# Layer two's expert tiles in a new order on three engines, and four of the eight gather buffers in other columns

## The reference

```python
logits = x @ router_w                        # 32 experts
probs = softmax(logits); topw, topi = top_k(probs, 4)
combine[t, topi] += topw / sum(topw)
g = einsum('th,ehi->eti', x, w_gate)         # 256 -> 96 per expert
u = einsum('th,ehi->eti', x, w_up)
routed = einsum('eti,te,eih->th', silu(g) * u, combine, w_down)
return shared + routed                       # shared: a dense two-layer branch
```

## Time and profile before

| | |
|---|---|
| median of three runs | 428.37 us |
| lowest and highest | 427.02 and 430.78 us |
| span of the profiled execution, first to last instruction | 462.5 us |
| TensorE busy | 421.1 us, 91% |
| VectorE, ScalarE, GpSimd busy | 329.8, 234.4, 216.2 us |
| first gate/up to the end of the tiles of layer two | 294.76 to 385.09 us |

### The profile page before, as it was taken

One profiled execution on the slowest core, in us unless ns is written; L12 is line 12 of the kernel. 1 busy time (PEld: TensorE's weight loads), 2 busy tenths in 40 slices (PEclk: granted clock), 3 DMA queues, 4 the chain that ended last, 5 costly groups with the idle time before them and its releaser, 6 DMA issues.

```text
span 462.5 us, 10086 instructions
## 1 busy us (share of the span) xinstructions
PE 421.1 (91%) x3213; PEld 327.6 (71%) x3213; DVE 329.8 (71%) x1135; ACT 234.4 (51%) x596; POOL 216.2 (47%) x208
## 2 busy tenths in 40 slices
PE   8899999899999998998989899958988999969696
PEld 4757899798999997656666684646766774645585
DVE  5886699978866667588999988525576664344685
ACT  3373233434433436878899636315566568124421
POOL 2023688767643320778880101655576602747400
PEclk9999999999999999589999999979999999979889
DMA  8937888888999982379776760233555523323202
GB/s 246 409 142 240 319 275 268 250 258 279 282 312 308 316 277 69 79 195 211 150 172 187 268 210 7 85 87 114 166 145 149 165 92 116 107 63 104 68 23 68
DMA packets 42274, 84.17 MB, mean 182 GB/s; under 512 B 7136, under 2 KB 27104, under 8 KB 41584
## 3 DMA queue, kind: packets, MB, share of 16 engines
q1 hardware_dynamic: 30656, 60.99, 39.6%
q0 software_dynamic: 9936, 20.85, 18.5%
q10 hardware_dynamic: 1632, 1.71, 1.1%
HBM read 65.81 MB, written 15.60 MB: 176 GB/s over the span
## 4 chain that ended last, share of the span: by engine, by line
PE 63%; DVE 14%; issue 8%; ACT 6%; another core or an unknown queue 4%; DMA 3%; SPq 1%; POOL 1%; ACTq 0%; DVEq 0%
PE ps L1169 14%; PE ps L1120 7%; PE ps L1185 7%; PE ps L1147 4%; PE ps L1289 4%; PE ps L964 3%; PE ps L1264 3%; PE ps L1106 3%; PE ps L1377 3%; ACT til L835 2%; PE ps L948 2%; PE ps L967 2%; DMA experts<-in_gu 2%; PE ps L1158 2%
## 5 line engine op out<-in xcount | busy, mean ns | idle before, releaser
L544 POOL DMA_INDIRECT til<-xn_rows,gidx x71 | 71.0, 999 | 98.1 <-PE ps L1158 43.4
L1169 PEld LDWEIGHTS ps<-til,experts 128*128 128x128 f32 x752 | 90.6, 192 | 8.1 <-issue 3.9
L1169 PE MATMUL ps<-til,experts 128*128 128x128 f32 x752 | 92.1, 276 | 3.2 <-DVE til L1645 1.5
L708 ACT ACTIVATE til<-ps 128x256 f32<-128x256 f32 x47 | 18.0, 382 | 66.2 <-PE ps L1158 66.2
L835 ACT ACTIVATE til<-til,mxs 128x128 f32<-128x128 f32 (+1 forms) x128 | 49.0, 453 | 0.0
L1185 PE MATMUL ps<-experts,til 128*128 x188 | 48.4, 381 | 0.0
L1120 PE MATMUL ps<-experts,til 128*64 x192 | 36.1, 345 | 9.4 <-issue 9.4
L756 ACT ACTIVATE til<-ps,wtile 128x256 f32<-128x256 f32 x95 | 42.0, 471 | 2.5 <-PE ps L1149 2.4
L1769 DVE CUSTOM_DVE_ANT_0 til<-ps,cst 128x128 f32<-128x128 f32 (+1 forms) x128 | 37.8, 352 | 5.7 <-PE ps L1264 3.3
L1120 PEld LDWEIGHTS ps<-experts,til 128*64 128x64 f32 x192 | 26.7, 144 | 15.5 <-issue 12.2
L1122 PE MATMUL ps<-xn,til 128*64 128x192 f32 x192 | 36.2, 345 | 0.0
(11 more groups left out here) (240 smaller groups left out, 959.4 us busy)
## 6 DMA issues: line engine op xcount, KB each, us to landing
experts<-in_gu SPq DMA_DIRECT2D x47, 512.0 KB
sorted_rows<-til SPq DMA_DIRECT2D x95, 128.0 KB
experts<-in_gu SPq DMA_DIRECT2D x8, 768.0 KB
experts<-in_dn SPq DMA_DIRECT2D x4, 1024.0 KB, 11.0
experts<-in_dn SPq DMA_DIRECT2D x8, 384.0 KB
experts<-att SPq DMA_DIRECT2D x44, 32.0 KB
til<-xn_rows,gidx POOLq DMA_INDIRECT x71
xr<-in_x SPq DMA_DIRECT2D x2, 512.0 KB, 4.2
```

Source lines behind the costliest of these rows:

```text
L544: po.indirect_dma_start(to, None, xn_dram[s.n], bass.IndirectOffsetOnAxis(ap=gidx[:, t:t + 1], axis=0))\
L1169: mm = pe.matmul(ps[:, b0, m * P:(m + 1) * P], gw[:, j, k * w + m * P:k * w + (m + 1) * P], xgT[:, j % 2, k, :], start=(k == 0), stop=(k = ...
```

## The change

Three things are changed.

- TensorE's order. The list is replaced by a loop that is written out: in step g gate/up of g, turn of g+1, down of g-1, the registers of g+1, turn-hidden of g. Beside before, T(g+1) and D(g-1) change places, and the register load moves behind D.
- The lists of ScalarE and VectorE. ScalarE's turn copies now run one group ahead, right behind the `silu` of the group; both weighings and both down copies stand together. VectorE makes the down copies and adds the biases ahead of the group's products of gate and up.
- The four gather buffers in `wqkv_sb` are given up. Tiles 4 to 7 of each eight go to the mask's columns of `cst`, to `bias_bf`, to `lgt` and to a new tensor `xg_more` of 1 KB per partition. Gather 4 waits for two counts of the block before (`s_wo`, `s_mx`) in place of `wide_done`.

```diff
-        xg1 = [xg[:, n, :] for n in range(4)] + [wqkv_free[:, n * D:(n + 1) * D] for n in range(4)]
+        xg1 = [xg[:, n, :] for n in range(4)]
...
+        xg_more = sb("xg_more", [P, D])
...
+        xg1 += [cst[:, C_MASK:C_MASK + D], bias_bf.bitcast(f32)[:, 0:D], lgt[:, :], xg_more[:, :]]
...
-                    if 0 <= g - lag < NT1 // 4:
+                    if max(0, -lag) <= g - lag < NT1 // 4:
                         work(g - lag)
...
                         if t == 4:
-                            po.wait_ge(s.wide_done, NTT)
+                            po.wait_ge(s_wo, BATCH)
+                            po.wait_ge(s_mx, 2 * BATCH * HEADS)
...
-                    run_double_tiles([(0, turn_four), (1, copy_second), (2, weigh_second), (0, gate_four), (2, silu_rows), (1, weigh_first), (0, copy_first)])
+                    turn_four(0)
+                    run_double_tiles([(2, weigh_second), (1, copy_first), (1, copy_second), (2, silu_rows), (0, gate_four), (-1, turn_four), (1, weigh_first)])
...
-                    run_double_tiles([(0, experts_of_four), (0, turn_four), (1, turn_h_four), (0, up_four), (1, down_four)])
+                    groups = NT1 // 4
+                    experts_of_four(0)
+                    turn_four(0)
+                    for g in range(groups):
+                        up_four(g)
+                        if g + 1 < groups:
+                            turn_four(g + 1)
+                        if g >= 1:
+                            down_four(g - 1)
+                        if g + 1 < groups:
+                            experts_of_four(g + 1)
+                        turn_h_four(g)
+                    down_four(groups - 1)
...
-                    run_double_tiles([(0, first_copies), (1, turned_four), (0, gate_four), (0, copy_four), (1, biases), (3, products)])
+                    run_double_tiles([(0, first_copies), (1, turned_four), (1, copy_four), (1, biases), (0, gate_four), (3, products)])
```

More of the change, by code:

```diff
@@ L167, in build_program @@
         gu_second = [xn_free[:, n * 384:(n + 1) * 384] for n in range(4)]
-        wqkv_free = wqkv_sb[:, :, :].rearrange("p k n -> p (k n)")
-        xg1 = [xg[:, n, :] for n in range(4)] + [wqkv_free[:, n * D:(n + 1) * D] for n in range(4)]
+        xg1 = [xg[:, n, :] for n in range(4)]
         dn_second = [wo0_sb[0:F1, n, :] for n in range(2)] + [xn_free[0:F1, 1536 + n * D:1536 + (n + 1) * D] for n in range(2)]
```

## The result

The changed kernel takes 430.46 us (median of 20 runs, 427.75 to 436.19); the kernel before took 428.40 us in the 20 runs beside it (425.84 to 432.33). The ratio is 1.0047 (1.0030 to 1.0065): slower by 2.0 us, 1.3 to 2.8. That is inside the range given, and on the other side of no change than the forecast. It is less than the 1% that the prediction took as what a measurement can tell from no change; with 20 runs of each, the interval tells it from no change all the same.

What follows compares the result with a forecast made beforehand. It took late TensorE signals, 0.91 to 0.94 us in each of eight layer-two groups, as the loss in the profile, mostly absent when timed. 428.4 - 1.1 - 1.0 + 0.2 = 426.5 us; range 419.2 to 432.5.

Steps and rivals of the forecast that it cites:

- the opening: Start of layer two's tiles: gathers 4 to 7 start sooner without the projections' wait; 1.0 us won, bounds 0 and 2.4.
- the freezes: TensorE's signals of finished tiles 1.5 us late beside gathers in layer two, costing 0.91 to 0.94 us a group.
- Nothing is added or removed: TensorE's order in layer two's groups: turn and down only change places, so the swap itself adds no time.
- The steady gain: Layer two's eight steady groups: gap ahead of gate/up closes, 7.4 us at full price, 1.1 at share 0.15.
- the 34.1 us between profile and clock: Profiled span 462.5 us against 428.37 timed; taken as mostly unexplained time that timed runs lack.
- Rival B: Layer two's groups: the freezes are real in full in timed runs, giving 420.2 us; chance 0.27.
- C: Layer two's gathers: real freezes, more of them with continuous gathers; 435.7 us, or 432.8 at six tenths; chance 0.12.
- rival E: Whole kernel: no effect, the end and gate/up's other wait take back the opening's 1.0; 428.4 us; chance 0.08.
- ScalarE's list: Weighings and down copies behind turn copies: hidden in groups, 0.2 us lost at the last down, bounds 0 and 0.8.
- VectorE's list: Biases and down copies ahead of the product turn-hidden needs; they fit ahead of gate/up's silu, so nothing.
- Rival D: Layer two's groups: gathers become the bound, 8.0 us a group if all are long, 444.9 us; chance 0.03.
- A: Whole kernel: the forecast itself, 426.5 us, own range 424 to 428.5; chance 0.50.

Runs made afterwards that it cites:

- e4: Kernel before with only the new gather buffers and the waits for gathers 4 to 7; ratio 0.9983 (0.9950 to 1.0015).
- e9: Kernel before with only the new gather buffers and waits, run a second time; 428.24 us, ratio 0.9995 (0.9971 to 1.0019).
- e2: Changed kernel with down put back ahead of turn on TensorE, new lists and buffers kept; ratio 1.0009 (0.9978 to 1.0041).
- e1: Kernel before, unedited, profiled once more; ratio 0.9999 (0.9967 to 1.0031), span 428.1 us.
- e7: Changed kernel again, unedited; 431.06 us, ratio 1.0068 (1.0037 to 1.0100).
- e3: Changed kernel with the old gather buffers and the old wait for the projections, new orders kept; ratio 1.0084 (1.0052 to 1.0116).
- e5: Changed kernel with TensorE's turn and down in halves of two tiles, down first; ratio 1.0045 (1.0014 to 1.0075).
- e6: Changed kernel with TensorE's turn and down in halves of two tiles, turn first; ratio 1.0105 (1.0073 to 1.0138).
- e10: Changed kernel a third time, unedited, on the same chip as e9; 431.41 us, ratio 1.0065 (1.0037 to 1.0093).

## Why the prediction was right or wrong

**The sum.** Two more changes of the array's use in each of ten groups cost 10 x 0.24 = 2.4 us, the tail 0.6, and the opening gives back 1.3: +1.7 us against 2.0 measured (1.3 to 2.8). By e4 and e9 the opening's gain may be less in the timed runs, which puts the sum between 1.7 and 3.0. A long gather 3 would add 1.4 in the executions that have it, and the agreement doesn't exclude some of those. I had -1.9: of the 3.9 us between that and the result, 2.4 are the changes of the array's use, 1.1 the freezes that weren't there and 0.4 the tail; the opening gave 0.3 more than expected. That leaves 0.3 unexplained, which is inside the interval.

**The step that failed** is the first of the parts, "Nothing is added or removed", for T ahead of D on TensorE. I counted instructions, and these are indeed the same; I took "D and its change-over" as one block that changes its place. But a change-over belongs to a pair of neighbours, not to a block. The old order has one behind D and one ahead of U, and none between U and D; the new one has two more, between U and T and between T and D. The trace of before had the price in it: the distance from the last gate/up to the first down and that from the last down to the first turn differ, and I read only starts of stages there. In numbers the term was 0 and is 2.4 us. Without it the traces sum to 1.3 - 0.6 = 0.7 us faster, the direction of the forecast; e2 is that kernel, and its times (1.0009, 0.9978 to 1.0041) can't be told from no change. TensorE has no idle time in these groups that could take it up, so it went to the time in full.

The Trainium skill has the rule: "TensorEngine Tiling (Array Packing)", section "Key Properties", says that changing the tiling mode, and not just the tile, drains TensorE. The traces agree in that each such change costs 0.12 to 0.15 us; that it is a drain no row shows. I hadn't weighed it, and it speaks against this change.

**The steady gain.** Expected 1.1 us from freezes paid at 0.15, with 0 and 7.4 as ends. Measured: none, as the second trace of before has groups of 5.98 us. The inference from the 34.1 us between profile and clock was right in kind, and its end 0 was the true one. What I set wrong was to take a trace that differed by 34 us as a picture of the kernel with a share to be scaled, when it was another kind of execution altogether. Against e1 its 34.4 us more are 6.2 ahead of T(0), 14.6 in the tiles (90.33 and 75.72) and 13.6 behind them (77.4 and 63.8). Rival B (0.27) falls for all usual executions, and so does C, which needed real freezes: its side came true, by another mechanism. That the result lies inside the whole range is luck for the same reason: what lies above 428.5 in it stands there for C's price, which nobody paid. The time lies 2 us above the forecast's own range (424 to 428.5) and nearest to rival E, no effect (428.4); E's reasons, that the end and another wait of U take the opening's gain back, hold for the tail only. By the page of the Trainium skill that the prediction cites here, "NOTIFIC — the notification-queue block", section "Overflow: three behaviours, one of which stalls the engine", the writing of records can stall an engine, which gives share 0. The share 0 came true, but no row shows this cause: e1 was recorded in the same way and has no freezes.

**The opening.** Expected 1.0, from 0.7 to 1.4; 1.3 in the traces. The step was right: the landing left the path. Gather 4 came 1.36 us behind gather 3 in e7 and e9, as worked out (1.06 and 0.30), in place of 3.76. But it then took 2.1 us itself where 0.94 was assumed, so gather 7 started 6.27 us behind gather 3 in e9 and 7.52 in e1, 1.25 us sooner and not 2.4. That was still enough for the wait of 1.2.

**ScalarE's list.** Hidden in the steady groups, as said (e2). The tail: bounds 0 and 0.8, 0.2 taken, 0.58 measured. I had argued that TensorE has only H(11) to cover it, which was the reason to stay near the upper end; I took the lower without a row.

**VectorE's list.** Taken as nothing. So it is in the steady groups. In the tail its down copies stand behind the copies of the hidden rows, end 0.05 us later than ScalarE's, and are what the last down waits for. By these two times either list alone should give nearly all of the 0.58; no run has only one of them.

One reading was off without consequence: the turn copies start at 363.90, 0.8 us and not 0.7 after T's last matmul began (363.08, the next row at 363.19 less 0.11).

**Rival D**, gathers as the bound: no. POOL is busy for 4.71 us of 6.23, and the gathers are as long as in the old order.

**The signs.** T stands right behind U and D behind T: seen. Groups of 6.0 us: 6.22. Second silu late: no, since there are no freezes. A span near 454 beside times near 426.5 as a sign for A: 427.2 beside 430.5, because a sign that rests on the trace of one odd execution has no worth for the next.

## What to carry to other kernels

When stages change places on an engine, count the borders between them as well as the stages: here every border between matmuls on part of the array and on the whole costs 0.12 to 0.15 us, though TensorE shows as busy throughout, so stages of one kind stand best side by side, and a reorder that closes an idle time must win more than its borders. Before a row of a trace is read, hold its span against the timed runs; where they differ by more than a few us, take another trace first, since a share of a rare event can't be scaled. At the end of a pipeline, where the cover runs out, list for every engine what stands ahead of the last wait.

## What the runs showed of the hardware

**A gather of two lengths.** Gather 3 starts while VectorE is in an unbroken train of sixteen fp16 products (279.78 to 283.35 in the changed kernel). In GpSimd's timeline of that trace, gathers 3 and 4:

```profile
280.71 3.46 POOL L546 DMA_INDIRECT til<-xn_rows,gidx  x1 [0.30 <-issue]
284.48 0.95 POOL L546 DMA_INDIRECT cst<-xn_rows,gidx  x1 [0.30 <-issue]
```

In e7, the same program, the same two:

```profile
283.12 1.05 POOL L546 DMA_INDIRECT til<-xn_rows,gidx  x1 [0.30 <-issue]
284.48 2.11 POOL L546 DMA_INDIRECT cst<-xn_rows,gidx  x1 [0.30 <-issue]
```

Either gather 3 takes 3.46 us or gather 4, where it is issued there, takes 2.11; both end 0.8 us behind the end of the train (283.35; in e7 285.76). When it is the third, T(0) waits for its landing, as TensorE's timeline of the changed kernel has it, and the way from T(0) to U(0) is 4.6 us in place of 2.69:

```profile
285.91 0.66 PE L1109 MATMUL ps<-cst,til 128*128 128x128 f32 x4 [1.71 <-DMA til<-xn_rows,gidx]
```

It was long in five of eight traces with new lists or a new order (the changed kernel, e3, e5, e6, e10) and in none of four without. With one program showing both, a chance of the single execution is enough to explain this; whether the new program makes it likelier stays open. That the products are what blocks it was not tried: only the place and the common end speak for it. The Trainium skill, "SBUF — State Buffer", section "SBUF: two separate sides", has an exclusive lock between VectorE and GpSimd that is held for a whole instruction. The trace would fit such a lock only in part: the wait lasts for a train of instructions of 0.23 us each (1.82 / 8), not for one.

**The clock ahead of the tiles.** In the attention before layer two the granted clock falls to half (1.2 GHz) for a while in most executions, and for how long varies. The same 14 us in the changed kernel (1.00), e1 (0.51) and e9 (0.76), windows, columns as above:

```profile
183.00:197.00 14.00, 12.15 (x155) 8.35 (x149) 12.52 (x70) 14.00 (x42) 9.69 (x7) 1.00 0.63 144
```

```profile
183.00:197.00 14.00, 13.43 (x97) 8.75 (x97) 9.27 (x53) 10.42 (x29) 11.15 (x8) 0.51 0.57 140
```

```profile
183.00:197.00 14.00, 11.84 (x116) 7.96 (x116) 10.25 (x60) 12.45 (x37) 9.21 (x7) 0.76 0.48 121
```

T(0) starts at 281.88, 285.84 and 285.58 in them, a spread of 4 us. Not all of it is the clock's: e9 had already waited 1.70 us for expert weights at 53.31, where e1 waited 0.20 at 51.08. The spread is twice what the change did, so spans of single traces can't rank these kernels: the changed kernel's 427.2 is shorter than e1's 428.1 though it is slower. The comparison above starts each stage at its own first instruction for that reason.

**The odd execution.** What held up the signals of TensorE in the first trace of before isn't known. None of the eleven traces taken later, with the same gathers at the same places, has it.
